# A metaformer block on one core: new orders around the whole scores, relative values ahead of both weighted sums

## Time and profile before

| | us |
|---|---|
| median of 3 runs | 145.8 |
| lowest and highest of them | 144.13 and 145.92 |
| the profiled execution | 143.62 |
| its span, first to last instruction | 141.8 |
| PE busy | 100.4 (71%) |
| DVE busy | 97.1 (69%) |
| ACT busy | 69.9 (49%) |
| POOL busy | 63.1 (44%) |
| mean granted TensorE clock | 0.934 of full |

### The profile page before, as it was taken

One profiled execution on the slowest core, in us unless ns is written; L12 is line 12 of the kernel. 1 busy time (PEld: TensorE's weight loads), 2 busy tenths in 40 slices (PEclk: granted clock), 3 DMA queues, 4 the chain that ended last, 5 costly groups with the idle time before them and its releaser, 6 DMA issues.

```text
span 141.8 us, 4291 instructions
## 1 busy us (share of the span) xinstructions
PE 100.4 (71%) x1830; PEld 69.2 (49%) x1830; DVE 97.1 (69%) x151; ACT 69.9 (49%) x150; POOL 63.1 (44%) x70
## 2 busy tenths in 40 slices
PE   0798995899189405988519986597857888999200
PEld 0332321288089305977419976441322347999100
DVE  5998838057203599815900399898999779888992
ACT  7958668900055023599234011616243389999300
POOL 8995928840000074995320056995640000006930
PEclk9999999999999975899965999999999999999975
DMA  4892994889910000023556100000000000000767
GB/s 149 274 251 27 208 205 94 186 172 243 212 15 5 5 0 0 0 62 88 146 126 156 45 5 0 7 0 5 0 0 0 0 0 0 5 2 0 199 188 205
DMA packets 9823, 11.63 MB, mean 82 GB/s; under 512 B 2828, under 2 KB 6924, under 8 KB 9804
## 3 DMA queue, kind: packets, MB, share of 16 engines
q1 hardware_dynamic: 9228, 10.31, 29.0%
q10 hardware_dynamic: 576, 1.05, 3.2%
HBM read 2.97 MB, written 2.10 MB: 36 GB/s over the span
## 4 chain that ended last, share of the span: by engine, by line
DVE 31%; PE 16%; SPq 14%; ACT 13%; POOL 10%; DMA 8%; issue 6%; ACTq 0%; DVEq 0%; POOLq 0%
SPq L291 7%; PE ps L998 6%; ACT warm L653 5%; PE ps L1046 4%; SPq L278 4%; DMA v_tile<-u_tile 4%; DVE xin L343 4%; DVE att_tile L742 3%; DVE stat L690 3%; PE ps L1023 3%; DVE y_tile L349 3%; POOL y_tile L422 3%; POOL y_tile L428 2%; DMA xin<-in_x_dram 2%; DVE u_tile L784 2%
## 5 line engine op out<-in xcount | busy, mean ns | idle before, releaser
L349 POOL TENSOR_TENSOR y_tile<-xin,u_tile 128x256 f32<-128x256 f32 (+1 forms) x7 | 7.1, 1052 | 24.0 <-DVE xin L343 24.0
L399 POOL TENSOR_TENSOR att_tile<-att_tile,soft 128x1024 f32<-128x1024 f32 x4 | 7.7, 1934 | 19.8 <-DVE soft L748 19.8
L1046 PE MATMUL ps<-spread,v_tile 128*32 128x64 f32 x512 | 10.8, 252 | 7.3 <-DMA spread<-rel_tile 4.5
L1046 PEld LDWEIGHTS ps<-spread,v_tile 128*32 128x32 f32 x512 | 10.0, 129 | 8.1 <-DMA spread<-rel_tile 4.8
L590 ACT ACTIVATE square<-y_tile 128x512 f32<-128x512 f32 x8 | 5.0, 630 | 15.4 <-POOL y_tile L422 15.4
L892 DVE TENSOR_SCALAR ps<-att_tile,bnv 128x512 f32<-128x512 f32 x15 | 11.0, 807 | 1.6 <-ACT warm L653 1.6
L784 DVE TENSOR_TENSOR u_tile<-ps,u_tile 128x512 f32<-128x512 f32 x8 | 5.4, 677 | 9.5 <-PE ps L1046 9.4
L1100 PE MATMUL ps<-blank 128*128 128x512 bf16 x48 | 11.2, 379 | 0.6 <-DVE u_tile L784 0.6
L967 PE MATMUL ps<-xin 128*128 128x512 f32 x18 | 11.5, 781 | 0.0
L1057 PE MATMUL ps<-rel_tile,w_bd 128*128 128x512 f32 x16 | 8.3, 621 | 3.3 <-DVE rel_tile L815 2.4
L405 POOL TENSOR_TENSOR att_tile<-att_tile,soft 128x1024 f32<-128x1024 f32 x4 | 7.7, 1928 | 5.8 <-DVE soft L754 5.8
(11 more groups left out here) (107 smaller groups left out, 235.4 us busy)
## 6 DMA issues: line engine op xcount, KB each, us to landing
out_dram<-y_tile SPq DMA_DIRECT2D x8, 256.0 KB, 2.4
xin<-in_x_dram SPq DMA_DIRECT2D x3, 512.0 KB, 4.8
spread<-att_tile SPq DMA_DIRECT2D x12, 128.0 KB, 2.5
v_tile<-u_tile SPq DMA_DIRECT2D x12, 128.0 KB, 2.4
spread<-rel_tile SPq DMA_DIRECT2D x24, 64.0 KB, 2.1
xin<-in_x_dram SPq DMA_DIRECT2D x2, 256.0 KB, 2.8
spread<-u_tile SPq DMA_DIRECT2D x4, 128.0 KB, 2.3
v_tile<-u_tile ACTq DMA_DIRECT2D x4, 128.0 KB, 4.6
```

Of the source, the lines that this page charges most:

```text
L349: return eng.tensor_tensor(result[:, :, rows, :], back[:, at:at + P * k].rearrange("p (q i j) -> p q i j", q=Q, i=k), x2[:, :, rows, :], A ...
L1046: ins = nc.tensor.matmul(ps[group(g), first + j // 8, at:at + Q * HALF].rearrange("p (q i) -> p q i", q=Q), v_t[:, j, g, :], att_bd[:, :, ...
```

## The change

In the order of the engines:

- SP loads gamma and beta before it spreads y 0, and regroups u 2 before it spreads y 3.
- PE projects u 1 before the relative factor, and computes the half product right behind u 3 into bank 3; ACT copies the halves of u 1 before it scales the turned Wv, and computes `first_beta` before it issues the DMAs of u 3. The scores wait for `first_beta` at j = 12.
- DVE takes maximum 2 and weight sum 0 before score sum 3, and all weight sums follow. DVE itself multiplies the weights of tile 3 (`weigh`), POOL no longer does; POOL shifts scores 2 before it weighs 0, and scores 3 before it weighs 1.
- Values and relative values use bank n for piece n, in place of banks 6 and 7 in turn. Values no longer wait for copies; relative value n waits for value copy n.
- All relative values come ahead of both halves of the weighted sums; the first half then waits for four relative outputs, the second for eight. DVE takes all relative outputs in one row in front of residual 0.
- ACT takes exponential 2 ahead of the value copies and spaces the others and the turned weights differently.
- Behind the sums, DVE does residuals 6 and 7 earlier and batch-norm parts later, POOL centres 6 before it scales 4, and ACT takes the Wx copies and squares in another order.

The core of the diff:

```diff
+            for k, a in enumerate((gamma, beta)):
+                sp.dma_start(affine[:, k:k + 1], bass.AP(a.tensor, 0, [[0, G], [1, C], [1, 1]])).then_inc(S["affine_in"], 16)
             spread_y(0)
...
             spread_y(2)
+            regroup_u(2)
             spread_y(3)
-            regroup_u(2)
...
             shift_scores(0)
             shift_scores(1)
+            shift_scores(2)
             weigh(0)
-            shift_scores(2)
+            shift_scores(3)
             weigh(1)
-            shift_scores(3)
             weigh(2)
-            weigh(3)
...
             centre(5)
+            centre(6)
             scale(4)
-            centre(6)
...
             def value_out(n):
                 act.wait_ge(S["value_product"], n + 1)
-                nc.scalar.copy(v_tile[:, BANK * n:BANK * (n + 1)], side_bank(n)).then_inc(S["value_ready"], 1)
+                nc.scalar.copy(v_tile[:, BANK * n:BANK * (n + 1)], bank(n)).then_inc(S["value_ready"], 1)
...
             turn_y(1)
+            u_half(1, 0)
+            u_half(1, 1)
             act.wait_ge(S["turned"], 1)
...
             ln_std(3)
-            u_half(1, 0)
-            u_half(1, 1)
...
             act.wait_ge(S["u_half"], 2 * Q)
+            act.wait_ge(S["half_product"], 1)
+            act.wait_ge(S["affine_in"], 32)
+            nc.scalar.activation(first_beta, ps[:, 3, 0:1], ACT.Identity, bias=affine[:, 1:2], scale=0.5).then_inc(S["first_beta"], 1)
...
             score_exp(0)
             score_exp(1)
+            score_exp(2)
             value_out(0)
+            turn_weights(0)
             value_out(1)
             value_out(2)
-            turn_weights(0)
+            score_exp(3)
             value_out(3)
+            turn_weights(1)
             value_out(4)
-            score_exp(2)
             value_out(5)
-            turn_weights(1)
+            turn_weights(2)
             value_out(6)
             value_out(7)
-            score_exp(3)
-            turn_weights(2)
+            turn_weights(3)
             spread_att(5)
-            turn_weights(3)
             spread_att(7)
...
+            def weigh(n):
+                dve.wait_ge(S["weight_recip"], n + 1)
+                nc.vector.tensor_tensor(att_m[:, n, :, :], att_m[:, n, :, :],
+                                        soft[:, 1, n, :].unsqueeze(2).broadcast_to([P, C, C]),
+                                        ALU.mult).then_inc(S["weights_dve"], 1)
...
             score_add(2)
+            score_max(2)
+            weight_sum(0)
             score_add(3)
-            weight_sum(0)
-            score_max(2)
+            score_max(3)
             weight_sum(1)
-            score_max(3)
             weight_sum(2)
-            relv_out(0)
-            relv_out(1)
             weight_sum(3)
-            relv_out(2)
-            relv_out(3)
+            weigh(3)
+            for n in range(PIECES4):
+                relv_out(n)
...
             residual(0)
-            relv_out(4)
-            relv_out(5)
             residual(1)
-            relv_out(6)
-            relv_out(7)
...
             project_u(0)
             keep_warm(2, 2)
+            project_u(1)
             relative_factor()
-            keep_warm(2, 2)
-            project_u(1)
-            keep_warm(2, 1)
+            keep_warm(2, 3)
             project_u(2)
             project_u(3)
+            pe.wait_ge(S["w_set"], G)
+            pe.wait_ge(S["ones_set"], 1)
+            nc.tensor.matmul(ps[:, 3, 0:1], w_bd[:, 2, :], ones[:, :], start=True, stop=True).then_inc(S["half_product"], 1)
...
             for n in range(PIECES4):
                 project_values(n)
             pe.wait_ge(S["rv_set"], 1)
-            for n in range(0, 4):
+            for n in range(PIECES4):
                 relative_values(n)
+            pe.wait_ge(S["relv_ready"], PIECES4 // 2)
             pe.wait_ge(S["att_in0"], 16 * Q * G)
             weighted_sums(0, range(C)).then_inc(S["wsum_product"], 1)
-            for n in range(4, 8):
-                relative_values(n)
+            pe.wait_ge(S["relv_ready"], PIECES4)
             pe.wait_ge(S["att_in1"], 16 * Q * G)
-            pe.wait_ge(S["first_beta"], 1)
-            weighted_sums(1, range(0, HALF))
-            pe.wait_ge(S["relv_ready"], PIECES4)
-            weighted_sums(1, range(HALF, C)).then_inc(S["wsum_product"], 1)
```

More of the change, by code:

```diff
@@ L314, in _ @@
             spread_y(2)
+            regroup_u(2)
             spread_y(3)
-            regroup_u(2)
             for g in range(G):
                 sp.dma_start(rv_in[group(g), :], rv.rearrange("c h i -> c (h i)")).then_inc(S["rv_in"], 16)
-            for k, a in enumerate((gamma, beta)):
-                sp.dma_start(affine[:, k:k + 1], bass.AP(a.tensor, 0, [[0, G], [1, C], [1, 1]])).then_inc(S["affine_in"], 16)
             for k in (0, 1, 2, 3, 4, 6):
@@ L506, in turn_weights @@
             def turn_weights(n):
-                act.wait_ge(S["weights"], n + 1)
+                if n < CHUNKS - 1:
+                    act.wait_ge(S["weights"], n + 1)
+                else:
+                    act.wait_ge(S["weights_dve"], 1)
                 act.wait_ge(S["score_sum"], n + 1)
@@ L758, in relv_out @@
                 dve.wait_ge(S["relv_product"], n + 1)
-                nc.vector.tensor_tensor(x2[:, :, rows, :], side_bank(n).rearrange("p (i q j) -> p q i j", i=ROWS, q=Q),
+                nc.vector.tensor_tensor(x2[:, :, rows, :], bank(n).rearrange("p (i q j) -> p q i j", i=ROWS, q=Q),
                                         xin[:, :, rows, :], ALU.add).then_inc(S["relv_ready"], 1)
+            def weigh(n):
[3 more added lines that the diff above has]
+                                        ALU.mult).then_inc(S["weights_dve"], 1)
             score_add(0)
@@ L839, in _ @@
             t_turn(0)
+            residual(6)
+            residual(7)
             t_turn(1)
@@ L842, in _ @@
             t_turn(2)
+            t_sum2(5)
             t_rstd(4)
-            t_sum2(5)
             t_turn(3)
             t_rstd(5)
-            residual(6)
-            residual(7)
+            t_sum2(6)
             bn_part(0)
-            t_sum2(6)
-            bn_part(1)
             t_rstd(6)
@@ L855, in _ @@
             t_rstd(7)
+            bn_part(1)
+            t_turn(5)
             bn_part(2)
[L857 to L858 removed]
             t_turn(6)
             t_turn(7)
+            bn_part(3)
             bn_part(4)
@@ L994, in scores @@
                     at = Q * C * (j % 4)
+                    if j == 12:
+                        pe.wait_ge(S["first_beta"], 1)
                     if j // 4 in SIDE and j % 4 == 0:
@@ L1028, in relative_values @@
                 half, row = n // 4, ROWS * (n % 4)
-                pe.wait_ge(S["weights"], 2 * half + 2)
-                if n < 2:
-                    pe.wait_ge(S["value_ready"], PIECES4 - 1 + n)
-                else:
-                    pe.wait_ge(S["relv_ready"], n - 1)
+                pe.wait_ge(S["weights"], 2 + half)
+                if half:
+                    pe.wait_ge(S["weights_dve"], 1)
+                pe.wait_ge(S["value_ready"], n + 1)
                 for k in range(ROWS):
                     for g in range(G):
-                        ins = nc.tensor.matmul(side_bank(n)[group(g), P * k:P * (k + 1)].rearrange("p (q j) -> p q j", q=Q),
+                        ins = nc.tensor.matmul(bank(n)[group(g), P * k:P * (k + 1)].rearrange("p (q j) -> p q j", q=Q),
                                                rv_t[group(g), ROWS * n + k, :], att_rows[group(g), half, :, row + k, :],
@@ L1079, in _ @@
             pe.wait_ge(S["w_set"], G)
-            pe.wait_ge(S["ones_set"], 1)
-            nc.tensor.matmul(ps[:, 4, 0:1], w_bd[:, 2, :], ones[:, :], start=True, stop=True).then_inc(S["half_product"], 1)
             for n in range(PIECES4):
```

22 lines of the change are left out of this document (7 added, 15 removed).

## The result

The changed kernel took 147.38 us (median of 4, 146.40 to 148.38) against 145.46 for the kernel before in the same session (144.13 to 145.92). The ratio is **1.0201, 95% interval 1.0125 to 1.0277**: slower, where I had forecast 141.9 us and a chance of 0.05 for slower. Ratios here leave out disturbed executions, so they are not the quotients of the medians beside them. The profiled execution took 146.40 us with a span of 144.6 (before: 143.62 and 141.8).

The account below looks back on a forecast made before the run. No single engine bounds the kernel: a chain of waits, with DVE the bound from 80.2 to 112.3 us. Gains 1.4 + 2.3 less 0.1 made 3.6 us, giving 141.9 us; range 139.5 to 144.2.

Parts of the forecast that it names:

- The beginning: Before the scores: the reordered loads, projections and copies are covered, worth 0 (-0.6 to +1.0 us); scores start at 39.4.
- The softmax on DVE: Score sums and maxima: last sum ends at 57.45 instead of 54.73, so PE's values start at 57.5 instead of 55.3.
- A bank per piece: PE's values and relative values: no waits for paired copies; values through by 66.9, relative values by 74.1 to 74.7.
- rival (a): Covered gain: the sums' start slips and scores start up to 1 us late; price 1 to 2.5 us, chance 0.22.
- The sums: Weighted sums: first half starts at 74.4, takes 4.35 us at full clock instead of 6.17, ends at 78.75; gain 1.4 us.
- DVE behind it: After the sums' first half, up to the aggregate: four relative outputs leave; 29.8 us instead of 32.1, gain 2.3 us.
- DVE and POOL at once: Centring 7 and normalising 7 on DVE come near a POOL operation's end: 0 to 1 us cost, 0.1 booked.
- The sum: Whole kernel: 1.4 + 2.3 - 0.1 = 3.6 us gain, span 141.8 to 138.2, forecast median 141.9 us.
- My rival for slower: PE's clock stays at 1.2 GHz, first sums end at 88 to 96, kernel takes 151 to 159 us; chance 0.05.

Follow-up runs that it names:

- the experiment above: Changed kernel with the softmax order nearly as before (score sum 3 ahead of weight sum 0, POOL weighing 0 and 1 early): 144.06 us, ratio 1.000 to the kernel before.
- the 29 small products: Changed kernel with two of three warming products replaced by 29 small ones, shifting PE's later stream by 54 records: 145.36 us, ratio 1.017 to the kernel before.
- ACT's two units held back: Kernel with softmax and late orders undone and 29 small products, ACT issuing weight units 5 and 7 only behind the first half's landing: 141.18 us, ratio 0.977.
- the one with ACT's transfers held: Changed kernel with ACT issuing its weight units 5 and 7 only when all of the first half's have landed: 147.26 us, ratio 1.023 to the kernel before.
- the best one: Changed kernel with softmax order nearly as before, old orders behind the sums, and 29 small products for two warming ones: 142.24 us, ratio 0.989 to the kernel before.
- the one with both orders: Changed kernel with softmax order nearly as before and old orders behind the sums, no shift of PE's stream: 143.35 us, ratio 0.990 to the kernel before.

## Why the prediction was wrong, point by point

- **The beginning**: right. The scores start within 0.3 us of the forecast, all its moves are covered.
- **The softmax on DVE**: the step itself was right (values at 57.12, forecast 57.5), and so was the clock, back at full about 4 us after the restart. What failed is the conclusion that the later start would cost only 0.4 us at the sums: the order costs about 2% of the kernel (the experiment above).
- **A bank per piece**: values nearly as forecast (9.2 us, forecast 9.4). Relative values took 8.7 instead of 7.2 to 7.8; 0.9 of it is a pause for a block. The landing came at 75.6 instead of 74.0. Beside it stand ACT's transfers, earlier now, and one more packet among SP's issues; the part of each is not shown. Together the start of the sums is 1.3 us late. This is rival (a), which I had at 0.22.
- **The sums, the step that failed**: "half of a half took 2.16 us at full clock, a half 4.35 instead of 6.17". It measured 7.93, 3.6 us more. The size was scaled from one run of 128 records, and the idle time in front of that row, "1.15 <-issue", was left out. PE did work through and the clock was full, as I said; but at full clock it is the supply of instructions that bounds it. Before the change this was hidden: behind 4.55 us of idle time the half ran its 256 records without a pause, in 6.17 us at a mean clock of 0.63, which is faster than 7.93 at full clock with pauses. The half was to become 1.8 us shorter and became 1.6 us longer; with its later start, residual 0 came 3.35 us later than before the change, where the forecast had it 1.5 earlier.
- **DVE behind it**: the 2.3 us for four outputs came (9.2 instead of 11.5 us up to residual 4). The claim that the late swaps "only keep DVE fed" failed: they cost 1.6 to 1.8 us. The trace shows an idle PE, half clock and a root behind a copy there; how the cost divides among the three was not tried.
- **DVE and POOL at once**: centring 7 took 1.10 us instead of 0.69, which is 0.4 where 0.1 was booked. The 0.69 us of the earlier trace rows were not taken alone, as the row is called: POOL had a memset under way from 10.13 to 11.94 us, so it was not every POOL operation that slowed DVE.
- **The sum**: the sums start 1.3 us later than forecast (75.68, forecast 74.4), their first half takes 3.5 more up to residual 0 (83.61, forecast 78.8), and the stretch from there to the aggregate 1.6 more. That is 6.4 of the 6.45 us between the forecast aggregate (108.7) and the measured one (115.15). My rival for slower, a clock that does not come back, had nothing to do with it; none of my rivals named PE's instructions.

Not tried: whether the next block can be had earlier, and whether SP's long issues and slow landings are caused by the packets beside them. When the granted clock falls differs between executions (last section), and its share in the small differences between the kernels is open.

## What to carry to other kernels

Before scaling a matmul's time, divide the whole stretch by its records, pauses included, and look for "issue" in front of rows that come after 128 records: a stream of small matmuls at full clock can be bound by how fast its instructions arrive, and then a freed bank or a faster clock buys less than the scaled time promises. When an order is changed to feed one engine, check what PE has to do meanwhile, since PE came back at half clock here after idling 3.25 us, and what stands in ACT's queue behind a copy that waits for it. Judge each swap of a bundle by itself: here two of the orders lost together what the rest of the change could give, and undoing them, together with the 29 small products and ACT's two units held back, made the kernel 2.3% faster than before.

## What the runs showed of the hardware that I had not expected

- PE's instructions come in blocks of 256, and idle time does not store more than about one block ahead: in the changed kernel no packet came between 47.5 and 62.8 us, while PE idled from 47.2 to 57.1, and no kernel here ran more than 256 small records at the sums behind an idle time without a pause. From one pause's end to the next were 3.5 to 4.0 us in the sums of the changed kernel.
- A block's packet and a DMA issue of 1.05 to 1.8 us instead of 0.59 go together on SP's queue (changed kernel and the one with ACT's transfers held). With ACT silent, transfers issued 0.3 to 0.6 us in front of a packet landed 2.6 to 3.5 us after their issue, where those away from a packet took 1.9 to 2.5. Both are coincidences in time, not tried as causes.
- The clock can fall in the first idle time in front of the scores in one execution and not in another: the scores took 8.1 us in the changed kernel and in the best one, 9.5 in the one with both orders.
- One matmul of 128 stationary columns in place of four of 32 made the same product slower, 14.3 us instead of 9.2, at mean clocks of 0.81 and 0.78.
